# A two-layer state-space network: layer 2's scans moved to tiles of 4 states x 32 channels

## The reference

```python
dbl = xc @ x_proj_w.T                      # xc: the branch's 128 channels
dt, Bm, Cm = dbl[..., :4], dbl[..., 4:20], dbl[..., 20:36]
dt = softplus(dt @ dt_proj_w.T + dt_proj_b)
def step(h, inp):                          # h: 128 channels x 16 states
    dA = exp(dt_t[..., None] * A)
    h = dA * h + (dt_t * x_t)[..., None] * B_t[:, None, :]
    return h, einsum('bds,bs->bd', h, C_t)
y = ys + xc * D_param
```

## Time and profile before

| | |
|---|---|
| time, median of 3 runs | 25599.84 us (25597.26 to 25621.22) |
| the profiled execution | 25619.33 us, its span 25617.4 us |
| granted TensorE clock, mean | 0.971 |
| busy over the span | PE 86%, DVE 88%, ACT 79%, POOL 85% |
| layer 1's scans | first scan at 1104.1 us, last at 17643.9 us |
| layer 2's scans | first scan at 20101.39 us, last product at 25047.72 us |

### The profile page before, as it was taken

How to read it: one execution, slowest core, us unless ns; L and a number is a source line. 1 busy time by engine, 2 the same in 40 slices (tenths; PEclk the granted TensorE clock), 3 DMA queues, 4 the chain that set the end, 5 groups by cost and what they waited for, 6 DMA issues and landing times. The chain is left out here.

```text
span 25617.4 us, 324037 instructions
## 1 busy us (share of the span) xinstructions
PE 22156.9 (86%) x104192; PEld 10130.7 (40%) x104192; DVE 22642.5 (88%) x20425; ACT 20191.0 (79%) x33916; POOL 21821.4 (85%) x10038
## 2 busy tenths in 40 slices
PE   8788888888888888888888888888899888888888
PEld 3344444444444444444444444443344333333332
DVE  8899999999999999999999999997511699999995
ACT  2499999999999999999999999995223566666662
POOL 1499999999999999999999999995012699999994
PEclk9899999999999999999999999999999999999999
DMA  6544444444444444444444444445423577777779
GB/s 204 189 104 113 114 102 108 116 104 108 116 107 104 115 110 103 110 113 104 112 115 104 109 116 103 107 116 155 145 89 104 181 229 230 230 229 230 230 231 297
DMA packets 1411313, 3654.68 MB, mean 143 GB/s; under 512 B 213364, under 2 KB 218488, under 8 KB 1306648
## 3 DMA queue, kind: packets, MB, share of 16 engines
q1 hardware_dynamic: 1310376, 3284.72, 45.4%
q10 hardware_dynamic: 99248, 349.22, 4.0%
HBM read 2781.87 MB, written 851.51 MB: 142 GB/s over the span
## 5 line engine op out<-in xcount | busy, mean ns | idle before, releaser
L887 DVE TENSOR_TENSOR_SCAN p_h<-p_dA,p_state,p_x_ps 128x512 f32<-128x512 f32 x10752 | 12853.5, 1258 | 356.5 <-PE p_x_ps L597 324.0
L850 POOL TENSOR_TENSOR p_hc<-p_h,p_c_sb 128x1536 f32<-128x1536 f32 (+1 forms) x3072 | 11743.8, 3825 | 138.9 <-PE p_y_ps L629 115.6
L597 PE MATMUL p_x_ps<-p_ident,p_scaled 128*128 128x128 f32 x49152 | 7802.9, 288 | 2201.3 <-DVE p_h L887 2005.5
L597 PEld LDWEIGHTS p_x_ps<-p_ident,p_scaled 128*128 128x128 f32 x49152 | 5336.6, 143 | 7870.9 <-DVE p_h L887 5393.6
L746 ACT ACTIVATE p_dA<-p_delta_rep,p_negA 128x512 f32<-128x512 f32 x12288 | 7991.4, 713 | 546.9 <-DVE p_h L887 536.9
L735 ACT ACTIVATE p_scaled<-p_duT,p_rowsT 128x384 f32<-128x384 f32 x11264 | 5908.4, 604 | 24.1 <-issue 0.4
L1596 DVE TENSOR_TENSOR_SCAN s_h<-s_dA,s_state,s_dbu 128x512 f32<-128x512 f32 x3056 | 3727.8, 1255 | 0.0
L1518 POOL TENSOR_TENSOR s_dbu<-s_du,s_b_sb 128x1024 f32<-128x1024 f32 x1537 | 3590.5, 2359 | 3.9 <-DVE s_h L1596 2.0
L629 PE MATMUL p_y_ps<-p_hc,p_fold 128*32 128x512 f32 x24576 | 3442.8, 634 | 151.5 <-POOL p_hc L850 149.7
L835 POOL TENSOR_TENSOR p_scaled<-p_duT,p_rowsT 128x1536 f32<-128x1536 f32 x1280 | 3533.3, 2760 | 5.6 <-ACT p_duT L722 5.6
L1431 ACT ACTIVATE s_dA<-s_delta,s_negA 128x512 f32<-128x512 f32 x3072 | 2023.0, 682 | 952.6 <-DVE s_h L1596 952.3
(11 more groups left out here) (197 smaller groups left out, 21510.5 us busy)
## 6 DMA issues: line engine op xcount, KB each, us to landing
s_b_sb<-rows SPq DMA_DIRECT2D x769, 1024.0 KB, 9.8
p_delta_rep<-delta SPq DMA_DIRECT2D x3072, 256.0 KB, 5.2
p_c_sb<-rows SPq DMA_DIRECT2D x1024, 256.0 KB, 4.8
p_u<-U SPq DMA_DIRECT2D x256, 768.0 KB
delta<-p_delta SPq DMA_DIRECT2D x256, 768.0 KB, 3.3
Y<-p_yo ACTq DMA_DIRECT2D x256, 768.0 KB, 4.2
s_c_sb<-rows SPq DMA_DIRECT2D x192, 1024.0 KB, 13.5
p_prev<-Y SPq DMA_DIRECT2D x128, 768.0 KB, 6.8
```

The lines of the kernel that those rows point to most:

```text
L597: last = pe.transpose(x_ps[:, tile % INPUTS, b * 128:(b + 1) * 128], scaled[:, x % 2, b, n % NJ * NI + i, :, :].rearrange("p r c -> p (r c ...
L850: pool.tensor_tensor(hc[:, n % 2, first:NI, :], h[:, n % H_RING, first:NI, :], c, ALU.mult).then_inc(hc_ready, 1)
L887: dve.tensor_tensor_scan(h[:, n % H_RING, i, :], dA[:, tile % DECAYS, :], x_ps[:, tile % INPUTS, :], initial, ALU.mult, ALU.add).then_inc( ...
```

## The change

`scan_phase` is replaced by `branch_scans`, layer 1's layout fitted to 128 channels. A unit is still 512 positions of a branch, and has 16 tiles of 4 states x 32 channels in 4 steps of 4 tiles (x counts steps over all units, i the tiles of one).

- Removed: the broadcasts of B over 128 partitions, GpSimd's products du*B, the bf16 parts of B and C with their matmuls, the reload of weights in each unit, ScalarE's saves of the states.
- Added: `turn_du`, `take_du`, `take_rows`, the scalings `scale` (16 states in each unit, of which ScalarE takes 1, 1, 1, 2 by step, each as four activations of 128 elements, and GpSimd 11, each 128x512), `turn_input` (64 transposes of 128x128 in a unit), delta's way through DRAM (`store_delta`, `spread_delta`), state copies on GpSimd.
- Moved: VectorE multiplies 2, 2, 2, 1 tiles of the four steps by C, in one instruction after the step's four scans, and GpSimd the other 2, 2, 2, 3. x_proj, rows, dt and softplus are done three units ahead, one of them in each step. They share the single buffer `prep_ps` with `turn_du` of two units ahead.
- Rings: 8 decays, 4 inputs in PSUM, 4 steps of states, 2 of products, 4 of scaled inputs; one buffer for C in PSUM.

```diff
-                decay, given = dA[:, (n * J + j) % DECAYS, :], dbu[:, i % AHEAD, j, :]
-                pool.tensor_tensor(dbu[:, i % AHEAD, :, :], a, b, ALU.mult).then_inc(dbu_ready, 1)
+    DECAYS, INPUTS, H_RING, HC_RING, X_RING, REP, LONG = 8, 4, 4, 2, 4, 3, 4
+    BY_ACT = (1, 1, 1, 2)
+    OWN = (2, 2, 2, 1)
+    on_pe = dict(xproj=0, rows=1, dt=2, turn_du=3)
+    on_act = dict(take=1, rows=2, soft=3, turn_du=0, evacuate=2, store=3)
...
+            def turn_du(g):
+                pe.wait_ge(du_ready, g + 1)
+                pe.wait_ge(delta_ready, min(g + 2, units))
...
+            def turn_input(x, i):
+                tile = x * NI + i
+                if i == 0:
+                    pe.wait_ge(scaled_act, scaled_to(x + 1))
+                    pe.wait_ge(scaled_pool, x + 1)
+                wait(pe, scanned, tile - INPUTS + 1)
+                for b in range(QB):
+                    last = pe.transpose(x_ps[:, tile % INPUTS, b * 128:(b + 1) * 128], scaled[...], ident[:, :])
...
+            def c_broadcast(x):
+                wait(pe, own_ready, x)
+                pe.matmul(c_ps[:, 0, :], pick[:, x % NG, :], xd[x // NG % LONG][0:ROWS_BC, :], ...)
...
+            def state_sum(x):
+                if x % NG == 0:
+                    direct(g)
+                pe.wait_ge(hc_ready, x + 1)
+                pe.wait_ge(own_ready, x + 1)
+                for i in range(NI): ...   # fold, four tiles into four quarters
...
+            for x in range(-EARLY * NG, units * NG + 2):          # TensorE
+                if ahead: turn_input(x + 1, 0)
+                if 0 <= x - 2 < units * NG: state_sum(x - 2)
+                if ahead: turn_input(x + 1, 1)
+                # by m: xproj(g+3), turn_rows(g+3), dt(g+3), turn_du(g+2)
+                if ahead:
+                    turn_input(x + 1, 2)
+                    c_broadcast(x + 1)
+                    turn_input(x + 1, 3)
...
+            for x in range(-EARLY * NG, (units + 1) * NG):        # ScalarE
+                # decay(x+1, 0..3), scale(x+3), then by m: take_xproj, take_rows, softplus (g+3),
+                # take_du(g+1), evacuate(g-1), store(g-1)
...
+            for x in range(-EARLY * NG, units * NG + 1):          # GpSimd
+                # state copy and times_c(x-1), scale(x+3), at m == 1 take_du(g+2)
...
+                for r in range(R - BY_ACT[x % NG]):
+                    last = pool.tensor_tensor(scaled[:, x % X_RING, :, :, r, :], duT[...],
+                                              rowsT[...].unsqueeze(3).broadcast_to([128, QB, NI, 32]), ALU.mult)
...
+            for x in range(units * NG):                           # VectorE
+                for i in range(NI):
+                    scan(x, i)
+                times_c(x)
```

More of the change, by code:

```diff
@@ L902, in _ @@
                             times_c(g * STEPS + m)
[L905 to L989, removed]
@@ L1005, in scan_phase @@
[L1005 to L1012, removed]
@@ L1036, in scan_phase @@
[L1036 to L1047, removed]
@@ new lines, in branch_scans @@
+        dA = sb("dA", [128, DECAYS, T])
+        h, hc = sb("h", [128, H_RING, NI, T]), sb("hc", [128, HC_RING, NI, T])
+        state, yo = sb("state", [128, TILES]), sb("yo", [128, T])
+        x_ps, y_ps = pb("x_ps", [128, INPUTS, T]), pb("y_ps", [128, 2, T])
+        c_ps, prep_ps = pb("c_ps", [128, 1, T]), pb("prep_ps", [128, T])
+        const_in, D_ready, negA_ready = sem("const_in"), sem("D_ready"), sem("negA_ready")
+        loaded, c_in = [sem(f"loaded{q}") for q in range(LONG)], [sem(f"c_in{q}") for q in range(2)]
@@ L1128, in _ @@
[L1128 to L1158 removed]
+                wait(eng, c_in[g % 2], g // 2 * 16 * R)
@@ new lines, in _ @@
+            for g in range(LONG):
+                load(g)
+            store_delta(0)
+            spread_delta(0)
+            for g in range(-2, units):
+                if g + 1 >= 0 and g + 1 < units:
+                    store_rows(g + 1)
+                if 0 < g + 2 < units:
+                    store_delta(g + 2)
+                if g + 1 >= 0 and g + 1 < units:
+                    spread_c(g + 1)
+                if 0 < g + 2 < units:
+                    spread_delta(g + 2)
+                if g >= 0 and g + LONG < units:
+                    load(g + LONG)
@@ L1238, in begins @@
-            def begins(g, s):
-                return s == 0 and not opens(g) and not folds(g)
-            def c_broadcast(g, s):
-                n = g * NS + s
-                if s == 0:
-                    pe.wait_ge(bc_ready, g * 3 + 3)
-                wait(pe, hc_ready, n)
-                for r in range(ng if in_product(s) == J else max(ng - 1, 1)):
-                    last = pe.matmul(c_ps[:, r, :], sel[:, s * ng + r, :], bc16[g % 2][:, :],
-                                     start=True, stop=True)
-                last.then_inc(c_done, 1)
@@ L1306, in _ @@
-            pe.wait_ge(D_ready, 1)
-            pe.wait_ge(const_in, 48)
-            pe.wait_ge(sel_ready, 1)
-            pe.wait_ge(minus_set, 2)
-            xproj(0)
-            for t in range(nd):
-                dt(0, t)
-            for part in range(2):
-                rest(0, part)
-            if NT:
-                turn_rows(0)
-                for t in range(nd):
-                    turn_du(0, t)
-            for g in range(units):
-                unit(g)
-            state_sum(units - 1, NS - 1)
@@ L1322, in _, with direct @@
-            for s in range(NS - LAG, NS):
-                if s in SHARE:
-                    pool_sum(units - 1, s)
+            def c_broadcast(x):
+                wait(pe, own_ready, x)
+                pe.matmul(c_ps[:, 0, :], pick[:, x % NG, :], xd[x // NG % LONG][0:ROWS_BC, :],
+                          start=True, stop=True).then_inc(c_done, 1)
+            def direct(g):
+                wait(pe, evacuated, g - 1)
+                pe.matmul(y_ps[:, g % 2, :], D_ident[:, :], u[g % LONG][:, :], start=True, stop=False).then_inc(direct_done, 1)
@@ new lines, in _ @@
+            pe.wait_ge(D_ready, 1)
+            for x in range(-EARLY * NG, units * NG + 2):
+                g, m = divmod(x, NG)
+                ahead = 0 <= x + 1 < units * NG
+                if ahead:
+                    turn_input(x + 1, 0)
+                if 0 <= x - 2 < units * NG:
+                    state_sum(x - 2)
+                if ahead:
+                    turn_input(x + 1, 1)
+                if g + EARLY < units:
+                    if m == on_pe["xproj"]:
+                        xproj(g + EARLY)
+                    if m == on_pe["rows"]:
+                        turn_rows(g + EARLY)
+                    if m == on_pe["dt"]:
+                        dt(g + EARLY)
+                if m == on_pe["turn_du"] and 0 <= g + 2 < units:
+                    turn_du(g + 2)
+                if ahead:
+                    turn_input(x + 1, 2)
+                    c_broadcast(x + 1)
+                    turn_input(x + 1, 3)
@@ L1482, in _ @@
-            act.wait_ge(sel_ready, 1)
-            scale_ident()
-            take_xproj(0)
-            if nd > 1:
-                for t in range(nd):
-                    take_dt(0, t)
-            softplus(0)
-            for part in range(2):
-                take_rest(0, part)
-            if NT:
-                take_rows(0)
-                for t in range(nd):
-                    take_du(0, t)
-            for g in range(units):
-                unit(g)
-            save_states(units - 1, GROUPS - 1)
@@ new lines, in _ @@
+            act.wait_ge(negA_ready, 2)
+            for x in range(-EARLY * NG, (units + 1) * NG):
+                g, m = divmod(x, NG)
+                if 0 <= x + 1 < units * NG:
+                    for i in range(NI):
+                        decay(x + 1, i)
+                if 0 <= x + 3 < units * NG and x + 3 >= NG:
+                    scale(x + 3)
+                if g + EARLY < units:
+                    if m == on_act["take"]:
+                        take_xproj(g + EARLY)
+                    if m == on_act["rows"]:
+                        take_rows(g + EARLY)
+                    if m == on_act["soft"]:
+                        softplus(g + EARLY)
+                if m == on_act["turn_du"] and 0 <= g + 1 < units:
+                    take_du(g + 1)
+                    if g + 1 == 0:
+                        for y in range(NG):
+                            scale(y)
+                if g and 0 <= g - 1 < units and m == on_act["evacuate"]:
+                    evacuate(g - 1)
+                if 0 <= g - 1 < units and m == on_act["store"]:
+                    store(g - 1)
@@ L1561, in _ @@
+            for x in range(-EARLY * NG, units * NG + 1):
+                g, m = divmod(x, NG)
+                if 0 <= x - 1 < units * NG:
+                    times_c(x - 1)
+                if NG <= x + 3 < units * NG:
+                    scale(x + 3)
+                if m == on_pool["du"] and 0 <= g + 2 < units:
+                    take_du(g + 2)
```

(34 more changed lines are left out.)

596 lines of the change are left out of this document (169 added, 427 removed).

## The result

The changed kernel takes 25285.43 us (median of 4 runs, 25261.63 to 25294.99), the kernel before beside it 25608.58 (4 runs, 25597.26 to 25621.22): ratio 0.9872 [0.9855, 0.9889]. The forecast was 25163 of 25599.8. The gain is 323 us, where 437 was expected. The profiled execution of after spans 25293.2 us.

What follows compares the result with a forecast made beforehand. VectorE bounds layer 2's scans before, GpSimd after: 192 units fall from 4938 to 4489 us (23.4 each), 449 less; minus 12 lost at the ends, 437 less, median 25163 us from 25599.8, range 25000 to 25310.

Steps and rivals of the forecast that it cites:

- VectorE's work: Layer 2's scans: 16 scans at 1.175 us plus products at 1.11 and 0.58, about 22.6 us a unit, the lower bound.
- GpSimd's work: Layer 2's scans: products, du, copies and 11 scalings at 0.99 us, 23.0 us a unit (22.0 to 25.5).
- The rival that the scaling costs what a product does: GpSimd's scaling at 1.22 us makes the unit 25.5, 25.9 with interlock: 47 us slower; chance 0.05.
- ScalarE's price and the ends: 128-element scaling 0.29 us; first scan 11 us later, 3 us stalls instead of 9.03, 6 at the end: net 12 lost.
- TensorE, step m = 2: TensorE's worst step, with dt and direct 2.1 us more; its sum runs 0.5 us over, within the slack.
- these 1.9: Slack in us on TensorE after VectorE's product frees the C buffer, until VectorE wants the next step's tile 3.
- Interlock: Loss from engines' lists waiting on each other: layer 1's 1.5% on GpSimd's 23.0, giving 23.4 us a unit.
- Which engine sets the pace: Layer 2's scans: GpSimd sets the pace, 25163 us, its own range 25080 to 25240; chance 0.58.
- The second rival: Waits of TensorE's list hold VectorE up by 6.4% as in layer 1: 24.05 us a unit, 25291 us; chance 0.20.

Runs made afterwards that it cites:

- e7: Changed kernel with `direct` (matmul with D) moved from step m = 2 to m = 1, GpSimd doing 10 scalings instead of 11, three product buffers: 25026.38 us, ratio 0.9771.
- e3: Changed kernel with TensorE's `direct` (matmul with D) moved from step m = 2 to the gap in m = 1: 25116.81 us, ratio 0.9803.
- e5: Changed kernel with three product buffers instead of two: 25119.83 us, ratio 0.9804.
- e8: Changed kernel with one redundant set of TensorE transposes of tile 2 added in step m = 1: 25108.66 us, ratio 0.9803.
- e4: Changed kernel with one more scaling per unit on ScalarE, GpSimd doing 10 instead of 11: 25283.57 us, ratio 0.9867.
- e1: Changed kernel with two redundant sets of TensorE transposes of tile 2 added in step m = 1: 25129.66 us, ratio 0.9804.
- e2: Changed kernel with two redundant sets of TensorE transposes added in step m = 3, where no gap stands: 25263.04 us, ratio 0.9864.

## Why the prediction was right in sign and some 120 us too low

**VectorE's work: right.** Scans 4.70/4 = 1.175 us from start to start, products 1.11 and 0.58; e7 shows the floor, 22.64 a unit against 22.6.

**GpSimd's work: right.** 1.007 us a scaling against 0.99, and a full unit of 23.11 to 23.13 in e3, e5 and e8 against 23.0. Of the difference the eleven scalings account for 11 x 0.017 = 0.19. The rival that the scaling costs what a product does falls with it. By the Trainium skill's rule on two inputs (GPSIMD Engine Reference, Performance versus the Vector engine) a scaling would have cost 1.25 us, an estimate from that page; this trace doesn't agree, 1.007 was measured, and the row of the same instruction with 1536 elements was the better guide.

**ScalarE's price and the ends: right enough.** Four scalings of 128 elements take 1.17 us (22001.92 to 22003.09), 0.29 each. The first scan came 9.2 us later, 11 was said. The stage end took 1.4 us more (6 said), and of the 8 us that the stage lost behind its first scan before, some 3 are left, as said: the first unit takes 26.8 us (20098.94 to 20125.76), the usual one 24.0. So the ends cost 9.2 + 1.4 + 3 - 8 = 5.6 us, not 12.

**TensorE, step m = 2: the step that failed.** The prediction let the sum there run "0.5 us past the step" and "eat part of these 1.9". Two things were wrong in it. It took every duration at full clock; measured, the stretch up to the sum took 4.57 us, not 2.93. And it measured the slack on the wrong consumer: tile 3 of the next step, wanted 3.5 us after the product, where the state sum two steps back has to end before VectorE's next product, one step's four scans (4.70 us) after. From the product's end at 22008.10, at full clock, that sum ends 0.14 + 2.93 + 1.0 = 4.07 us later, a slack of 0.63 and not 1.9. At the low clock it is 0.14 + 4.57 + 1.0 = 5.71 us, 1.0 too late, and VectorE waited 1.15. With the right consumer alone the plan would still have held, by 0.63 us; the clock is what broke it.

**Interlock: mis-sized through that.** 1.5% above GpSimd, 23.4 us, was carried over from layer 1; 24.03 was measured. From the first scan to the last product the forecast had 4489 us and 3 of stalls; 4614.1 were measured, 122 more. The start and the end outside this stretch took 10.6 us more than before, where 17 were forecast, 6 less. That leaves 116; the profiled execution was forecast at 25182 and took 25295, 113 more; the other 3 lie in the stages around. Where the wait is gone (e3, e5), GpSimd has no idle time at all and the lists cost it nothing, so layer 1's figure held for neither.

**Which engine sets the pace.** Not GpSimd, as forecast: e4 took 1 us a unit off it for nothing. The measured 25285 lies outside the 25080 to 25240 that the forecast gave this case, with a chance of 0.58. The second rival, VectorE held up by TensorE's list through the one C buffer, the one `prep_ps` and two product buffers, had the number (24.05 a unit, 25291) and most of the mechanism: VectorE's only wait is for a product buffer, TensorE's gap ahead of it is at the C buffer, and `prep_ps` plays no part in either. It was given 0.20, and its 6.4% from layer 1 had no clock in it, so that its number hit as well as it did is partly luck. What spoke for it in the profile, TensorE at 21.5 of 23.4 us with one C buffer, should have been worked out at both levels of the clock for the step with the least slack. GpSimd becomes the bound only when the sum is in time (e1, e3, e5, e8), and VectorE only when both are relieved (e7).

**Open.** Shown is that the low clock makes the sum late, and the late sum makes VectorE wait (the units of the changed kernel and of e2, and e1's 2.93 us). Why the clock falls isn't. That the place of TensorE's idle time counts is argued from e1 and e8 against e2. Neither a gap nor the idle time in all is enough: e5 has gaps of 1.27 us ahead of the sums and e7 one of 1.75 in nearly every unit, both at a mean clock of 0.98, and the kernel before, whose TensorE was idle more, with gaps of up to 1.37 us, ran the stage at full clock:

```profile
20200.00:24400.00 4200.00, 3758.19 (x9147) 1335.37 (x9145) 4200.00 (x3921) 2796.14 (x4738) 4038.45 (x2125) 1.00 0.72 230
```

Nor is a gap needed: in e1 the clock still fell in some units in m = 3, with no gap just ahead, as in this window of it:

```profile
22018.00:22020.00 2.00, 2.00 (x13) 0.65 (x11) 2.00 (x3) 1.97 (x3) 2.00 (x3) 0.51 0.17 67
```

e3 changes the gap and the work behind it together, so how its gain divides between the two isn't known.

## What to carry to other kernels

Where an in-order engine waits on a short ring, find for each ring the consumer whose slack is least, and price the chain to it at the low clock as well as at the full one: 0.63 us of slack at the full clock was a loss of 1.0 at the low one. An engine 97% busy need not be the bound; take a little work off it and look whether the time moves. And when a wait is short and regular, move real work into the gap or add a buffer; either recovered 166 to 169 us here, and both with a better split 259.

## What was unexpected in the hardware

TensorE, 93% busy over the stage, was granted 0.50 of its clock for some 3.4 us in nearly every unit of 24 us, 107 times in 2400 us, nearly always soon after its list had stood for up to 1.16 us at one place. Redundant transposes in that place made the kernel 156 us (two tiles a unit) and 177 us (one) faster. The kernel before left TensorE idle for 442 us of 4200 in the same stage, the changed one for 275, and only the changed one lost clock. On GpSimd a product of two full operands takes 1.22 us for 512 elements a partition and one with a second operand constant over 32 elements 1.007.
